# First attention of a gated cross-attention block: where the pairs of row maxima stand among the score and value tiles

## The reference, cut to what matters

```python
xn, ln_lat = layer_norm(ctx, g1, b1), layer_norm(_layernorm(x), g2, b2)
q  = ln_lat @ Wq
k, v = split(concatenate([xn, ln_lat]) @ Wkv, 2)
weight = einsum('bhld,bhnd->bhln', q * scale, k * scale)   # 16 heads, 2048 x 3649
weight = where(full_mask, weight, -max)
weight = softmax(weight, axis=-1)
x = x + tanh(g_xattn[0]) * (einsum('bhln,bhnd->bhld', weight, v) @ Wout)
```

## Time and profile before

| what | value |
| --- | --- |
| time before, median of 3 | 3395.67 us (3392.9 to 3396.04) |
| profiled execution: its own time | 3392.96 us |
| its span in the trace | 3391.1 us |
| busy over the span: TensorE, VectorE, GpSimd, ScalarE | 89%, 72%, 61%, 54% |
| P of the first attention (L713) | 2048 matmuls, first start 99.0 us, last 2298.7 us |
| V of the first attention (L753) | 3712 matmuls |

### The profile page before, as it was taken

One profiled execution on the slowest core, in us unless ns is written; L12 is line 12 of the kernel. 1 busy time (PEld: TensorE's weight loads), 2 busy tenths in 40 slices (PEclk: granted clock), 3 DMA queues, 4 the chain that ended last, 5 costly groups with the idle time before them and its releaser, 6 DMA issues. The chain is left out here.

```text
span 3391.1 us, 53618 instructions
## 1 busy us (share of the span) xinstructions
PE 3001.4 (89%) x21696; PEld 1101.4 (32%) x21704; DVE 2453.9 (72%) x3029; ACT 1817.4 (54%) x2033; POOL 2082.1 (61%) x968
## 2 busy tenths in 40 slices
PE   3589999999999999999999999998697799999947
PEld 1223333333333333333333333322354133333324
DVE  5567777778767877778777876782535888888758
ACT  3155445555555545544555555544443588888833
POOL 0077898888888889879888888989510111111022
PEclk9699999999999999999999999999698799999969
DMA  1000000000000000000000000000210100000000
GB/s 59 5 1 1 1 7 1 1 1 7 1 1 7 1 1 7 1 1 7 1 1 1 2 1 1 1 1 1 74 23 13 42 7 6 7 8 6 4 0 26
DMA packets 24536, 28.72 MB, mean 8 GB/s; under 512 B 6431, under 2 KB 21216, under 8 KB 24290
## 3 DMA queue, kind: packets, MB, share of 16 engines
q1 hardware_dynamic: 24290, 25.30, 2.6%
HBM read 17.42 MB, written 2.10 MB: 6 GB/s over the span
## 5 line engine op out<-in xcount | busy, mean ns | idle before, releaser
L413 POOL TENSOR_TENSOR a_acc_p<-a_acc_p,a_prob 128x1024 f32<-128x1024 f32 x704 | 1726.1, 2452 | 299.5 <-ACT a_prob L483 217.8
L543 DVE TENSOR_REDUCE a_part_max<-wide 128x2 f32<-128x1024 f32 x896 | 1088.4, 1215 | 475.6 <-PE wide L713 474.9
L483 ACT ACTIVATE a_prob<-slot,a_mask_bias 128x1024 f32<-128x1024 f32 x928 | 987.6, 1113 | 732.1 <-PE slot L738 712.7
L753 PE MATMUL bank<-a_prob,a_val 128*64 128x512 f32 x3712 | 898.8, 606 | 2.1 <-ACT a_prob L483 2.1
L713 PE MATMUL wide<-a_k_hi,a_q_hi 64*128 64x512 f16 (+1 forms) x2048 | 365.9, 369 | 147.4 <-DVE a_part_max L543 134.9
L1025 ACT ACTIVATE a_prob<-slot,a_mask_bias 128x1024 f32<-128x1024 f32 x416 | 455.4, 1116 | 65.5 <-PE slot L1183 52.2
L1067 DVE TENSOR_REDUCE a_part_max<-wide 128x1 f32<-128x512 f32 x514 | 332.7, 681 | 37.3 <-PE wide L1171 20.4
L753 PEld LDWEIGHTS bank<-a_prob,a_val 128*64 128x64 f32 x3712 | 226.6, 136 | 394.9 <-issue 290.2
L738 PE MATMUL slot<-a_q_hi,a_k_lo 64*128 64x512 f16 x1856 | 353.1, 377 | 0.0
L738 PE MATMUL slot<-a_q_hi,a_k_step_hi 64*128 64x512 f16 x1728 | 328.7, 377 | 2.6 <-ACT a_prob L483 2.5
L738 PE MATMUL slot<-a_q_lo,a_k_step_hi 64*128 64x512 f16 x1728 | 328.3, 377 | 0.0
(11 more groups left out here) (367 smaller groups left out, 3284.6 us busy)
## 6 DMA issues: line engine op xcount, KB each, us to landing
a_w_staged<-in_w SPq DMA_DIRECT2D x8, 384.0 KB, 3.2
x_res<-in_x SPq DMA_DIRECT2D x1, 2048.0 KB, 9.1
a_q_op<-a_hi SPq DMA_DIRECT2D x128, 16.0 KB, 1.8
out_x<-x_res SPq DMA_DIRECT2D x16, 128.0 KB
a_k_op<-mid_k_hi SPq DMA_DIRECT2D x32, 52.0 KB, 2.2
mid_context<-in_ctxt SPq DMA_DIRECT2D x1, 1601.0 KB, 6.6
mid_w_staged<-in_w1a SPq DMA_DIRECT2D x4, 385.0 KB, 4.2
ctx_rows<-in_ctx SPq DMA_DIRECT2D x1, 1536.0 KB
```

The costliest lines, as they stand in the source:

```text
L413: nc.gpsimd.tensor_tensor(acc, before, prob[:, k % R, :], ALU.add).then_inc(added_p, 1)
L483: nc.scalar.activation(prob[:, k % R, :], m.slot[k % 2][:, :], ACT.Exp, bias=mbias[:, t:t + 1]).then_inc(probs_ready, 1)
L543: nc.vector.reduce_max(part_max[:, w % 2, :, j, c], pairs, AX.X).then_inc(max_used, 1)
L753: ins = nc.tensor.matmul(av[r, :], val[g % 2][:, t, r], prob[:, k % R, h * QB:(h + 1) * QB], start=(t == 0), stop=(t == NT - 1), tile_posi ...
```

## The change

Only the order of calls on TensorE in that loop changes. Per two steps it becomes

```diff
                 for t in range(NT):
                     n = w * NT + t + a.lead
+                    scores(w, t)
                     if t % 2 == 0:
                         if n < S:
                             pair(n)
-                        scores(w, t)
                         continue
-                    scores(w, t)
+                    if t == 1:
+                        tiles = [(w - 1, NT - 2), (w - 1, NT - 1)] if w else []
+                    else:
+                        tiles = [(w, s) for s in range(t - 3, t if t == NT - 2 else t - 1)]
+                    for own in tiles[:1]:
+                        values(*own)
                     if n < S:
                         pair(n)
-                    if t == 1:
-                        for s in (NT - 2, NT - 1) if w else ():
-                            values(w - 1, s)
-                    else:
-                        for s in range(t - 3, t if t == NT - 2 else t - 1):
-                            values(w, s)
+                    for own in tiles[1:]:
+                        values(*own)
                     if w and t == a.sums_at:
                         sums(w - 1)
```

## The result

The changed kernel takes 3419.32 us, median of 4 runs (3417.84 to 3423.89), against 3394.98 us before: ratio 1.0075, 95% interval 1.0057 to 1.0092. It is slower by 24 us; forecast were 15.5 us more, 3408.5, with a range of 3392 to 3424. (The ratio is taken against four runs of the kernel before, the table ahead of the prediction against the first three of them.) The profiled execution's span is 3418.2 us, 27.1 longer than before.

What follows compares the result with a forecast made beforehand. TensorE's own work was taken as the bound, with about 5% of holes. 8 units of +0.30, 22 of +0.57 and +0.5 for the last part gave 15.5 us on 3392.96, so 3408.5; range 3392 to 3424.

Steps and rivals of the forecast that it cites:

- The stall goes: Plain rounds: one S and one V between two P take 1.73 us, above the maximum's 1.71, ending the 0.19 stall.
- The added layout changes cost 0.255 a round: Plain rounds: a second way into and out of V on TensorE costs 0.105 + 0.15 us; round 3.96 for 3.90.
- Rival 1: Plain rounds: only the way into V costs, 0.105 us a round more; 3366 us, or 3337 with both free; chance 0.12.
- Rival 3: V behind S and S behind V cost 0.15 us each way or more; 3424 us, at twice that 3440; chance 0.10.
- The 0.15 that I put on the way back: TensorE going from V back to S: taken as 0.15 us, the same as from V to P.
- Additions hide part of it: First units of head groups, steps 11 to 13 and 18 to 21: VectorE's 7.18, 5.48 and 5.79 us stay; cost 0.
- The copy of the old sum is covered: First V of a unit, step 3: ScalarE's copy fits under TensorE's work; cost 0, at most some 0.05 us a unit.
- TensorE's 1.77 us: TensorE's time from the old unit's last V to the new unit's first V: 0.15 + 0.645 + 0.225 + 0.645 + 0.10.
- Rival 2: VectorE or GpSimd catches TensorE in more rounds, so the extra 0.06 us a round hides; 3393 us; chance 0.12.

## Why the prediction was right, and where it was not

Right is the mechanism: the stall goes, and the added layout changes cost more than it gave. The size was too small, for two terms of the sum.

- *The stall goes.* Right. 0.19 us in a plain round, and gaps of 1.97 and 1.99 for 1.71 and 2.19.
- *The added layout changes cost 0.255 a round.* Right: 0.26 between the two orders with halved maxima. With the stall's 0.19 this leaves 0.06 a round. Rival 1 (one way free, 3366 us) is out. Rival 3 (dearer changes, 3424 us) cannot be ruled out by the time, which is nearer to it than to the forecast; the rows rule it out, with 0.31 from S to V and 1.01 from V to S, for its 0.35 and 1.05. The 0.15 that I put on the way back are 0.05 inside V and 0.10 behind it, which changes no sum here.
- *Additions hide part of it.* Half right. In steps 11 to 13 and 18 to 21 I took VectorE's spans over from before where it set them, and elsewhere in 18 to 21 took no wait at all. But beside GpSimd VectorE's additions have no length of their own: 1.2 to 3.4 us, by how they fall among GpSimd's, and a new order shifts that. Steps 18 to 21 came out 0.52 us a unit dearer, 10 to 13 0.13 cheaper. This is the term of the sum that was mis-sized most. With GpSimd's additions cut to 8 columns the P of step 21 comes at 1.97 in every unit.
- *The copy of the old sum is covered.* Wrong. I set it against TensorE's 1.77 us and forgot that on ScalarE it stands behind the projection of step 1. It cost 0.18 a unit on average; with the copy ahead, the changed kernel is 3412.9.
- *The size.* 15.5 forecast, 24 measured. In the trace 0.98 a unit stand against 0.50; the two terms give +0.57, the other steps together -0.09. The sign, the range and the main mechanism held. That the time lies inside the range is in part luck: the first unit gave back 5.1 us that the prediction did not have. Without them the time would be about 3424 (an estimate, 3419.3 + 5.1), the very edge of the range.
- *Rival 2 (nothing moves).* Out: TensorE sets the plain rounds in both orders.

Why VectorE's addition of step 19 falls on GpSimd's in three kinds of unit stays open. That it comes from the new spacing of the exponentials, as GpSimd's start at 1125.90 behind ScalarE suggests, was not tried by itself.

## What to carry to other kernels

Where blocks of matmuls with different layouts alternate, count the blocks: splitting one to even out a wait pays only if the wait is longer than one way in and one way out (here 0.255 us). Fill the longest holes first: here one V in a hole of 0.84 us gained 19 us, while the same move into holes of 0.19 lost. An operation that takes turns with another engine has no fixed duration, so a span that it sets cannot be carried over to a new order; bound it by its shortest and longest row.

## What the runs showed of the hardware

A change of the array's layout cost TensorE 0.10 us at full granted clock, with the type kept (0.31 for 0.215 between fp16 matmuls, 0.53 for 0.43 between fp32 ones) as with the type changed. Into the fp32 matmuls of V another 0.05 was lost between the first two pairs. The price of a V block was the same to 0.01 us behind S as behind P (0.31 and 0.32 from the start of the last 512-column pass to V; 1.01 from V to either).

VectorE's addition of two 128x1024 fp32 operands took 1.215 us with GpSimd nearly idle and up to 3.38 us beside GpSimd's additions of the same form. The added time stands in the trace as part of VectorE's own instruction, not as a wait ahead of it. GpSimd's additions were stretched too: 2.34 us the shortest in the kernel before, 3.37 the longest.

Two fills of the one PSUM tile `wide` could not follow each other closer than 1.70 to 1.72 us: 0.43 to the start of the maximum, 1.23 for it, 0.05 to the next P. With only one S between two P they still stood at 1.70 (S ahead of P in the even step only).
